# Attention on one Trainium2 core: two copies of the first block of queries moved from VectorE to ScalarE

## What is computed

```
s = einsum('bthd,bshd->bhts', q, k) * scale            # 16 query heads, 8 key heads, 2048 positions, 2 batches
logits = 2 * log(abs(s) + 1e-30) + log_G[t] - log_G[s], masked to s <= t
m = max(logits, axis=-1)
a = exp(logits - m), masked
num = einsum('bhts,bshd->bthd', a, v);  den = sum(a)
y = num / (den + 1e-06), then a layer norm over each head
```

## Time and profile before

| | us |
|---|---|
| median of 3 runs | 2032.64 (2031.67 to 2033.09) |
| the profiled execution | 2033.64 |
| its span | 2031.6 |
| PE busy | 1895.0 (93%) |
| DVE busy | 1760.0 (87%) |
| ACT busy | 1299.4 (64%) |
| POOL busy | 818.9 (40%) |

### The profile page before, as it was taken

One profiled execution on the slowest core, in us unless ns is written; L12 is line 12 of the kernel. 1 busy time (PEld: TensorE's weight loads), 2 busy tenths in 40 slices (PEclk: granted clock), 3 DMA queues, 4 the chain that ended last, 5 costly groups with the idle time before them and its releaser, 6 DMA issues. The chain is left out here.

```text
span 2031.6 us, 37336 instructions
## 1 busy us (share of the span) xinstructions
PE 1895.0 (93%) x12827; PEld 1340.2 (66%) x12827; DVE 1760.0 (87%) x2762; ACT 1299.4 (64%) x2204; POOL 818.9 (40%) x687
## 2 busy tenths in 40 slices
PE   7999859999999999999999996899938999999997
PEld 6677625555555555555555553799837999999997
DVE  5999849999999999999999998777677788878774
ACT  4544448778788878778887783344436656566553
POOL 3777611222221222122222211466615576656653
PEclk9999869999999999999999998899957999999999
DMA  5887794776655667665676612344452343344343
GB/s 183 282 291 266 253 271 101 176 162 156 147 127 136 157 161 176 135 150 131 137 171 161 161 53 77 93 133 130 117 172 71 81 94 71 83 89 92 76 96 61
DMA packets 169768, 288.61 MB, mean 142 GB/s; under 512 B 52592, under 2 KB 126721, under 8 KB 163137
## 3 DMA queue, kind: packets, MB, share of 16 engines
q1 hardware_dynamic: 143344, 247.64, 45.6%
q0 software_dynamic: 15360, 20.99, 6.6%
q10 hardware_dynamic: 10896, 17.83, 2.6%
HBM read 159.19 MB, written 100.27 MB: 128 GB/s over the span
## 5 line engine op out<-in xcount | busy, mean ns | idle before, releaser
L1034 ACT ACTIVATE att_sb_a<-att_ps_s,att_sb_fg,att_sb_f 128x1024 f32<-128x1024 f32 x384 | 456.9, 1200 | 201.5 <-PE att_ps_s L1204 160.5
L1074 DVE TENSOR_TENSOR keep_sb_store<-keep_sb_store,att_sb_a 128x1024 f32<-128x1024 f32 (+2 forms) x528 | 526.9, 1025 | 6.8 <-ACT att_sb_a L1034 6.2
L990 POOL TENSOR_SCALAR_AFFINE_SELECT att_sb_dec<-att_sb_dec 128x128 f32<-128x128 f32 x256 | 214.7, 841 | 763.7 <-ACT att_sb_dec L1024 763.7
L1223 PE MATMUL att_ps_off<-att_sb_a,att_sb_v 128*64 128x512 f32 x1520 | 363.2, 593 | 0.0
L1915 ACT ACTIVATE ffn_sb_h<-ffn_ps_p,ffn_sb_b_cols 128x256 f32<-128x256 f32 x320 | 151.8, 476 | 174.0 <-PE ffn_ps_p L2098 173.0
L1204 PEld LDWEIGHTS att_ps_s<-att_sb_q,att_sb_k 64*128 64x128 f32 x1896 | 159.2, 185 | 120.8 <-issue 54.1
L1204 PEld LDWEIGHTS att_ps_s<-keep_sb_late,att_sb_k 64*128 64x128 f32 x1920 | 160.8, 185 | 117.1 <-issue 49.7
L1204 PE MATMUL att_ps_s<-att_sb_q,att_sb_k 64*128 64x512 f32 (+2 forms) x1896 | 232.1, 375 | 5.6 <-DMA att_sb_k<-k_rows 4.2
L1204 PE MATMUL att_ps_s<-keep_sb_late,att_sb_k 64*128 64x512 f32 (+3 forms) x1920 | 235.2, 375 | 1.6 <-DVE att_sb_a L1090 1.1
L2014 DVE TENSOR_TENSOR ffn_sb_h_lo<-ffn_sb_h,ffn_sb_h_hi 128x256 fp32r<-128x256 f32 x320 | 200.0, 670 | 21.4 <-ACT ffn_sb_h_hi L1908 20.2
L1090 DVE SCALAR_TENSOR_TENSOR att_sb_a<-att_ps_s,att_sb_dec 128x1024 f32<-128x1024 f32 (+3 forms) x256 | 208.5, 814 | 4.2 <-PE att_ps_s L1204 2.0
(11 more groups left out here) (251 smaller groups left out, 3460.5 us busy)
## 6 DMA issues: line engine op xcount, KB each, us to landing
q_rows<-early_sb_halves SPq DMA_DIRECT2D x32, 1024.0 KB, 4.9
att_sb_k<-k_rows SPq DMA_DIRECT2D x60, 512.0 KB, 17.5
att_sb_tops<-keep_sb_store SPq DMA_DIRECT2D x240, 128.0 KB, 2.4
close_sb_nT<-num_rows SPq DMA_DIRECT2D x34, 512.0 KB, 4.0
k_rows<-early_sb_halves SPq DMA_DIRECT2D x16, 1024.0 KB, 5.1
keep_sb_late<-q_rows SPq DMA_DIRECT2D x32, 512.0 KB, 15.6
num_rows<-att_sb_num SPq DMA_DIRECT2D x64, 256.0 KB, 3.0
keep_sb_raw<-L_ffn_W ACTq DMA_DIRECT2D x32, 512.0 KB, 3.8
```

Of the source, the lines that this page charges most:

```text
L990: nc.gpsimd.affine_select(out=tile, in_=tile, compare_op=ALU.is_ge, fill=0.0, base=0, pattern=[[1, P]], channel_multiplier=-1).then_inc(de ...
L1034: nc.scalar.activation(x, s_ps[slot(op)][:, :, :], ACT.Square, scale=f[:, p, i - 1, s:s + 1], bias=fg[:, p, i - 1, s:s + 1]).then_inc(sq_d ...
L1074: nc.vector.tensor_tensor(x[:, :, c:TB], x[:, :, c:TB], y[:, :, c:TB], ALU.max).then_inc(max_done, 1)
L1223: last = nc.tensor.matmul(ps[h * HD:(h + 1) * HD, c:TB], v_tile, a[:, a_slot(op), h, c:TB], start=(s == 0), stop=(s == (ST * i if kind == ...
```

## The change

Both parts touch block 0 alone.

- `total` of block 0 (128x512, PSUM to SBUF) is now an ACT activation with the function Copy, in ACT's list at the key of the last values + 0.60. DVE's was at + 0.42.
- The copy of the first diagonal tile (128x1024) is gone from DVE. The maximum of the second tile, which covers columns 128 to 511 of each head, takes the first tile as its other operand instead of `acc`. What the second tile does not cover, columns 0 to 127 of each head, is copied by ACT (`corner`, 128x256) at the key of the first tile + 3.34, with a semaphore of its own, on which the mover of the maxima, the last transposes and the next user of the slot of `a` wait too. The first tile's slot is now released by the second tile's maximum, two places later than before.

```diff
+        if op[2:] == (0, 0):
+            return place[op[:3] + (1,)] + 5.69
         return place[op] + 5.7
...
+    act_todo += [(place[q, "diag", 0, 0] + 3.34, "corner", (q,)) for q in range(PAIRS)]
+    act_todo += [(values_at(last_own(q, 0)) + 0.60, "total", (q, 0)) for q in range(PAIRS)]
...
-    dve_todo += [(values_at(last_own(q, i)) + 0.42, "total", (q, i)) for q, i in owns]
+    dve_todo += [(values_at(last_own(q, i)) + 0.42, "total", (q, i)) for q, i in owns if i]
...
             def move(q, i):
                 sp.wait_ge(max_done, max_order.count(last_own(q, i)))
+                if i == 0:
+                    sp.wait_ge(corner_done, q + 1)
...
+            def corner(q):
+
+                op = (q, "diag", 0, 0)
+                act.wait_ge(sq_done, sq_order.count(op))
+                if q:
+                    act.wait_ge(moved[0], 16 * ST * q)
+                nc.scalar.activation(acc[:, 0, :, 0:P], a[:, a_slot(op), :, 0:P], ACT.Copy).then_inc(corner_done, 1)
+
+            def total(q, i):
+                n = total_order.rank[q, i]
+                act.wait_ge(av_done, av_order.count(last_own(q, i)))
+                act.wait_ge(num_st[n % 2], n // 2 * 16)
+                nc.scalar.activation(num[:, n % 2, :], own_ps[:, :], ACT.Copy).then_inc(num_done, 1)
...
-                if kind == "off" and s == 0:
+                if s == 0 and (kind == "off" or i == 0):
                     return
                 dve.wait_ge(sq_done, sq_order.count(op))
-                if q and s == (0 if i == 0 else 1):
+                if q and s == 1:
                     dve.wait_ge(moved[i], 16 * ST * q)
-                if kind == "diag" and s == 0 and i == 0:
-                    nc.vector.tensor_copy(x, y).then_inc(max_done, 1)
+                if kind == "diag" and s == 1 and i == 0:
+                    first_tile = a[:, a_slot((q, "diag", 0, 0)), :, :]
+                    nc.vector.tensor_tensor(x[:, :, c:TB], first_tile[:, :, c:TB], y[:, :, c:TB], ALU.max).then_inc(max_done, 2)
...
-                if i == 0:
-                    nc.vector.tensor_copy(num[:, n % 2, :], own_ps[:, :]).then_inc(num_done, 1)
```

More of the change, by code:

```diff
@@ L920, in attend @@
         moved = [m.sem(f"moved{i}") for i in range(NB)]
-        fold_done = m.sem("fold")
+        fold_done, corner_done = m.sem("fold"), m.sem("corner")
         prep_done, et_done, exp_done, dec_done = (m.sem(s) for s in ("prep", "et", "exp", "dec"))
@@ L930, in wait, with wait_corner @@
                 eng.wait_ge(sem, order.count(op))
+        def wait_corner(eng, op):
+            if op is not None and op[1:] == ("diag", 0, 0):
+                eng.wait_ge(corner_done, op[0] + 1)
         def arrived(eng, q):
@@ L1032, in square @@
                     wait(act, max_done, max_order, a_user(op))
+                    wait_corner(act, a_user(op))
                     act.wait_ge(s_done, s_order.count(op))
@@ L1050, in _ @@
                     query_factor(*op)
+                elif what == "corner":
+                    corner(*op)
+                elif what == "total":
+                    total(*op)
                 else:
@@ L1087, in own_scores @@
                 wait(dve, max_done, max_order, a_user(op))
+                wait_corner(dve, a_user(op))
                 dve.wait_ge(s_done, s_order.count(op))
@@ L1106, in total @@
                 dve.wait_ge(num_st[n % 2], n // 2 * 16)
-                if i == 0:
-                    nc.vector.tensor_copy(num[:, n % 2, :], own_ps[:, :]).then_inc(num_done, 1)
-                else:
-                    dve.wait_ge(part_done, part_order.count((q, i)))
-                    nc.vector.tensor_tensor(num[:, n % 2, :], part[:, et_order.rank[q, i] % 2, :], own_ps[:, :], ALU.add).then_inc(num_done, 1)
+                dve.wait_ge(part_done, part_order.count((q, i)))
+                nc.vector.tensor_tensor(num[:, n % 2, :], part[:, et_order.rank[q, i] % 2, :], own_ps[:, :], ALU.add).then_inc(num_done, 1)
             def fold(q, n):
@@ L1175, in scores @@
                         pe.wait_ge(max_done, max_order.count(last_own(q, i)))
+                        if i == 0:
+                            pe.wait_ge(corner_done, q + 1)
                         rows = acc[:, i, :, :].rearrange("p h c -> p (h c)")
```

## The result

The changed kernel takes 2038.44 us (median of 9 runs, 2037.12 to 2039.13), the kernel before 2033.09 (9 runs measured beside it): a ratio of 1.0023, 95% interval 1.0015 to 1.0032. It is 5.3 us slower (3.0 to 6.5 by the interval), although DVE is busy for 12 us less. The forecast was 2038.8, which is 6.2 over the kernel before.

A forecast was written before the change was run, and what follows sets the result against it. Bound: a ring of two saturated engines, PE and DVE, with little play. +7.0 (stall) + 1.0 (corner) - 1.0 (play used) - 0.8 (end) = +6.2 us; against 2032.64, 2038.8 us, range 2035 to 2042 (8 in 10: 2023 to 2043).

The forecast's parts named there:

- The stall: PE's values of the next diagonal block wait 1.5 us for ACT's `total`; 1.4 reaches DVE, in five pairs 7 us.
- The corner: ACT's `corner` ahead of the square of place 37 makes PE's weights of place 40 late: 0.2 us, 1.0 in five pairs.
- The other ten pairs: After pairs 3 and 4 and their like, ACT's `total` ends 0.6 and 0.4 us before PE needs it: no stall.
- The rival in which ACT gets in the way: Squares delayed 0.6 us in the other ten pairs reach PE or DVE: 5 us more, 2044; chance 0.08.
- What the relief gives: Gain limited to the play at PE's hand-over of scores to DVE (places 5, 13): 1 us in the steady state.
- The end: In the last pair DVE is the path: 0.60 us of the second copy and 0.2 of the first, 0.8 gained.
- on the part that PE carries: DVE's two copies, at places 38 and 46, lie where PE sets the rate, so their 1.29 us a pair mostly gains nothing.
- DVE alone as the bound: Rival: PE only follows DVE; 2012.0 us if the gain is whole, 2020.0 with the stalls, 2026.3 with half; chance 0.22.
- the stalls were not absorbed: Rival: PE regains half of the 8 us by losing its small waits at places 24 to 32: about 2034; chance 0.27.
- cost the same with another operand: The second tile's maximum keeps its 128x768 and its cost, so DVE's relief is 1.29 us a pair.
- the 60.0 us a pair of the start: Rate read from the copy of block 0's sum, first at 344.8 and last at 1245.0 us: 900.2 us over 15 pairs.
- DVE as the engine to relieve: The skill's rule, first rival: PE's weight loads fill only 102.52 of 200 us, so DVE alone is the bound; chance 0.22.

The follow-up runs named there:

- both moved: The changed kernel with ACT's `total` at key + 0.42 instead of + 0.60 and `corner` at + 4.20 instead of + 3.34: 2029.70 us, ratio 0.9982 to the kernel before.
- the copy done twice: The kernel before with DVE's 128x1024 copy done a second time, into a tile that nobody reads: 2040.43 us, ratio 1.0033 to the kernel before.
- one fold less: The kernel before without the first of three folds of the maxima (a 128x1024 DVE instruction at place 20.5): 2025.69 us, ratio 0.9962.
- both moved and one fold less: The changed kernel with `total` at + 0.42, `corner` at + 4.20 and the first fold of the maxima left out: 2024.11 us, ratio 0.9954 to the kernel before.
- the corner alone: The kernel before with only the merged maximum and ACT's `corner` at + 3.34, `total` staying on DVE: 2034.89 us, ratio 1.0007.
- `total` alone: The kernel before with only block 0's `total` moved to ACT at + 0.60, DVE keeping its 128x1024 copy: 2040.06 us, ratio 1.0033.

## Why the prediction was right, point by point

**The stall.** Forecast 1.5 us of PE in pairs 2, 5, 8, 11 and 14; measured 1.45 us of idle time after pair 5, and 7.2 us in five between 400 and 1200 us. Removing it by the order alone gave back 1.48 us in three pairs. The copy took 0.58 us against 0.59.

**The corner.** Forecast 0.2 us in the same pairs, measured 0.30: its step in full. I had let a small wait of PE's absorb a third of it, and it did not.

**The other ten pairs.** Forecast no stall; PE's waits for ACT's copy number five in 800 us, those of pairs 2, 5, 8, 11 and 14. They are the only five of the whole trace, so none of another kind of body has one. The rival in which ACT gets in the way there as well is out: these bodies take 60.06 and 59.71 us, against 60.08 and 60.01 before.

**What the relief gives.** Forecast, by kind of body, nothing after pair 4, 0.1 us after pair 5 (the play at place 13) and 0.2 after pair 3, where 0.2 was a guess at twice the 0.1; the version with both moved shows 0.02, 0.07 and 0.29, and 0.40 in three pairs against 0.3.

**The end.** The last reduction of the maxima stands at 1250.59 before and at 1256.92 after, so attention ended 6.33 us later (the sum said 6.2):

```profile
1250.59 1.23 DVE L1126 TENSOR_REDUCE keep_sb_row_max<-att_ps_s 128x8 f32<-128x1024 f32 x1 [0.65 <-PE att_ps_s L1183]
```

```profile
1256.92 1.22 DVE L1154 TENSOR_REDUCE keep_sb_row_max<-att_ps_s 128x8 f32<-128x1024 f32 x1 [0.65 <-PE att_ps_s L1213]
```

From the fifteenth pair's reduction to this last one it takes 29.72 us before (from 1220.87) and 28.87 after (from 1228.05): 0.85 came out at the end, forecast 0.8. The profiled spans differ by 2036.7 - 2031.6 = 5.1 only, since what follows attention, which the change does not touch, took 1.2 us less in this execution (779.8 after that reduction against 781.0). The medians say 5.35. That the forecast of 2038.8 and the measured 2038.44 are so close is in part chance: the median of before moved by 0.45 us between the two sets of runs, and the terms miss in opposite ways. In three pairs the corner was put 0.1 too low and the gain of the relief 0.1 too low as well, and the two cancel. The mechanism does not rest on that luck, the closeness does.

**Where the working was wrong.** The step on which, by its own words, everything rested holds only in part. The sentence that the two copies lie "on the part that PE carries" is half of the truth. Less DVE work there gives next to nothing, but more of it costs at once (the copy done twice). The path has a second course, by DVE through that stretch, on the mean only some 0.3 us a pair shorter, and after pair 5 and its like not shorter at all. It did not touch this forecast, since the change took work away; it would have spoiled one for a change that adds some.

Two smaller points. The maximum of the second tile does not cost the same with another operand: its step is 0.96 us against 0.87, so the relief was 1.20 us a pair and not 1.29, and nothing in the sum depends on it. And the 60.0 us a pair of the start is read from the first copy to the last, which takes in the end of the last pair; the bodies alone take 59.9, so three pairs went from 179.8 to 181.2.

**The rivals.** Of the rivals, DVE alone as the bound is excluded by three runs (both moved, one fold less, both moved and one fold less), and the stalls were not absorbed: the 1.48 us came back in full when their cause was taken away. That ACT delays the other ten pairs is excluded by the bodies above.

**DVE as the engine to relieve.** With some 2.4 us a pair taken from DVE the body gets 0.55 us a pair shorter, and then PE is busy with matmuls for 200.00 of 200 us and with weight loads for 103.74. The Trainium skill (Perfetto Trace Analysis, Identifying the Most-Contended Engine) goes for TensorE by the weight loads, and by MFU (the share of the engine's peak arithmetic rate that the kernel uses), which is not worked out here, and not by the matmuls' busy time. By the weight loads DVE was the engine to relieve. The runs disagree: PE was within 0.55 us a pair of its own pace with its weight loads at half the time. In this kernel the matmuls' busy time came nearer to telling the bound, though not without the experiment.

## What to carry to other kernels

Where two engines are both busy for 99% and neither waits, ask for the play in each hand-over, not for the busier engine: it bounds what a relief can give, here 0.13 us a pair of 1.29, though the same engine relieved at another place gave 0.48 of 1.14. And test it in both directions: play against less work says nothing of play against more. An instruction that moves to an engine with time to spare should be priced by what stands ahead of it in that engine's list and who waits for it; here the place in the list was worth 1.5 us at each of five places and its work nothing. And a moved instruction needs a price at both ends, the place it leaves and the place it comes to.

## What was not expected

POOL's select on the decay tiles (128x128) took 855 ns in the mean before, 731 with the change and 713 with the corner alone, but 873 with `total` alone. The DVE copy from SBUF to SBUF is gone in the two cases where it is shorter. It is no longer when that copy is done twice (860), and without one fold, with the copy in place, it is 723. So that copy alone is not the cause; which DVE instructions matter was not tried. The rows of 400 to 1200 us, of the kernel before and of the one with one fold less:

```profile
L990 POOL TENSOR_SCALAR_AFFINE_SELECT att_sb_dec<-att_sb_dec 128x128 f32<-128x128 f32 x213 | 181.8, 855 | 618.0 <-ACT att_sb_dec L1024 618.0
```

```profile
L990 POOL TENSOR_SCALAR_AFFINE_SELECT att_sb_dec<-att_sb_dec 128x128 f32<-128x128 f32 x215 | 155.3, 723 | 644.7 <-ACT att_sb_dec L1024 644.7
```

The merged maximum (128x768, the two operands both slots of `a`) takes 1041 ns at the median; the maxima of that width that read and write `acc` take 946 in the mean. And ACT's copy of 128x512 from PSUM costs ACT 0.48 us (from 647.74 to 648.22, where its next instruction starts) for a duration of 0.58, less than the 0.62 us step of an exponential of the same width from SBUF (645.27 to 645.89 in the earlier trace rows).
